# Other PSUM banks for the last rounds of a first attention, and its gate inputs normalised in two rounds

## The reference

```
x = x + xattn0(layernorm(x), ctx)    # 16 heads of 8, softmax over 128 keys, then wo and bo
x = x + ffn0(layernorm(x))           # 8 experts, top 2 of softmax(x @ gate_w)
x = x + xattn1(layernorm(x), ctx)    # 16 heads of 64, low-rank additions, 4 extra context tokens
x = x + ffn1(layernorm(x))           # 16 experts of 256, each takes its best 32 of 256 tokens
```

## Time and profile before

| | |
|---|---|
| time, median of 3 runs | 531.92 us (531.68 to 533.07) |
| profiled execution | 532.59 us, span 530.9 us |
| TensorE busy | 495.0 us, 93% of the span |
| VectorE busy | 397.5 us, 75% |
| ScalarE busy | 272.2 us, 51% |
| GpSimd busy | 235.7 us, 44% |
| first attention, rounds 12 to 17 | about 85 to 126 us of the span |

### The profile page before, as it was taken

One profiled execution on the slowest core, in us unless ns is written; L12 is line 12 of the kernel. 1 busy time (PEld: TensorE's weight loads), 2 busy tenths in 40 slices (PEclk: granted clock), 3 DMA queues, 4 the chain that ended last, 5 costly groups with the idle time before them and its releaser, 6 DMA issues.

```text
span 530.9 us, 13371 instructions
## 1 busy us (share of the span) xinstructions
PE 495.0 (93%) x5113; PEld 380.4 (72%) x5113; DVE 397.5 (75%) x1064; ACT 272.2 (51%) x728; POOL 235.7 (44%) x331
## 2 busy tenths in 40 slices
PE   5799998889999998999989999999999999999996
PEld 4467665546567776777768777778857897789895
DVE  6788998556687789777897897777986678536553
ACT  3366564445475564657545665555663544514332
POOL 5844553025365525556255454633312890081440
PEclk9699999899999999999999999999999999999999
DMA  8900000000001101111000000021110400001001
GB/s 227 220 4 4 2 2 2 2 1 7 4 0 32 32 2 33 32 32 32 2 2 1 3 1 3 3 62 45 39 41 1 120 1 2 0 4 41 2 2 41
DMA packets 21871, 14.47 MB, mean 27 GB/s; under 512 B 5928, under 2 KB 21136, under 8 KB 21808
## 3 DMA queue, kind: packets, MB, share of 16 engines
q1 hardware_dynamic: 20704, 13.31, 9.1%
q10 hardware_dynamic: 1104, 0.30, 0.3%
HBM read 12.30 MB, written 1.05 MB: 25 GB/s over the span
## 4 chain that ended last, share of the span: by engine, by line
PE 73%; DVE 20%; issue 3%; ACT 2%; DMA 1%; POOL 0%; SPq 0%; DVEq 0%
PE bank L1758 9%; PE bank L1767 5%; PE bank L1352 5%; PE bank L1521 5%; PE bank L1433 4%; PE bank L1528 4%; PE bank L1508 4%; PE bank L1690 4%; PE bank L1480 4%; PE bank L1500 4%; PE bank L1491 3%; PE bank L1774 3%; PE bank L1337 3%; PE bank L1579 3%; DVE negmax L756 2%
## 5 line engine op out<-in xcount | busy, mean ns | idle before, releaser
L496 POOL TENSOR_TENSOR work<-work,rsum 128x496 f32<-128x496 f32 x64 | 64.2, 1015 | 131.6 <-DVE rsum L774 131.6
L1128 ACT ACTIVATE work<-bank,negmax 128x124 f32<-128x124 f32 x256 | 72.7, 378 | 77.6 <-DVE ipa_s L758 77.6
L531 POOL TENSOR_SCALAR work<-work,slot 128x128 f32<-128x128 f32 x64 | 49.8, 804 | 48.1 <-DVE slot L849 29.3
L1758 PE MATMUL bank<-work 128*128 128x256 f32 x224 | 53.4, 381 | 0.0
L993 DVE SCALAR_TENSOR_TENSOR work<-work,bank 128x256 f32<-128x256 f32 x64 | 26.9, 420 | 32.9 <-ACT work L1280 32.7
L479 POOL TENSOR_TENSOR work<-work 128x512 f32<-128x512 f32 (+2 forms) x48 | 40.3, 839 | 14.1 <-DVE work L728 11.6
L1280 ACT ACTIVATE work<-bank 128x256 f32<-128x256 f32 x64 | 24.6, 384 | 40.5 <-PE bank L1758 29.0
L1758 PEld LDWEIGHTS bank<-work 128*128 128x128 f32 x224 | 40.3, 190 | 4.7 <-DVE work L996 0.2
L430 POOL TENSOR_TENSOR rstd<-veps,minus_half 128x1 f32<-128x1 f32 (+3 forms) x28 | 21.1, 754 | 49.3 <-DVE veps L573 49.2
L756 DVE TENSOR_REDUCE negmax<-bank 128x4 f32<-128x496 f32 x64 | 42.3, 662 | 0.0
L627 DVE TENSOR_REDUCE negmax<-bank 128x8 bf16<-128x1024 f32 x32 | 39.1, 1221 | 4.3 <-PE bank L1322 3.6
(11 more groups left out here) (197 smaller groups left out, 1086.3 us busy)
## 6 DMA issues: line engine op xcount, KB each, us to landing
work<-in_L_ffn_w_dram SPq DMA_DIRECT2D x42, 128.0 KB, 2.3
x_all<-in_x_dram SPq DMA_DIRECT2D x4, 256.0 KB, 5.5
out_dram<-x_all SPq DMA_DIRECT2D x4, 256.0 KB, 2.5
ctx_all<-in_ctx_dram SPq DMA_DIRECT2D x4, 192.0 KB, 5.7
ctx_all<-in_L_ffn_w_dram SPq DMA_DIRECT2D x6, 128.0 KB, 2.2
work<-in_L_xattn_Wq_dram SPq DMA_DIRECT2D x1, 512.0 KB, 6.4
work<-in_L_xattn_Wo_dram SPq DMA_DIRECT2D x1, 512.0 KB, 8.5
work<-in_L_ffn_We_dram SPq DMA_DIRECT2D x1, 512.0 KB, 6.0
```

The costliest lines, as they stand in the source:

```text
L496: pool.tensor_tensor(part, part, rsum1[:, b % 2, CH * n:CH * n + CH].unsqueeze(2).broadcast_to((128, CH, ORG)), ALU.mult).then_inc(Z.norm, 1)
L531: ins = pool.tensor_scalar(ohw_of(e)[:, k, :], count[:, :], slot[:, h, 0, k, e % E1:e % E1 + 1], slot[:, h, 1, k, e % E1:e % E1 + 1], ALU. ...
L1128: ins = act.activation(p1[:, b % 2, n, c, 0:ORG], blocks(bank[n])[:, c, 0:ORG], ACT.Exp, bias=negmax1[:, b % 2, CH * n + c:CH * n + c + 1])
L1758: mm = pe.matmul(halves(bank[4 + c])[:, n, :], up_weights(e, n, c), xgT[e // E1][:, :, e % E1, :], start=True, stop=True)
```

## The change

Spare rounds now go to 13 (SPARE 14). After them, round 14 uses bank 2 for both the turned maxima and the projection, round 15 bank 0, rounds 16 and 17 bank 7. values0 waits for VectorE's reads only in rounds 0 and 1. In exchange, TensorE waits ahead of project0 for the last user of each of these banks: in round 13 for ScalarE's copy of the turned gate inputs, in round 14 for the last maxima, in round 15 for the three copies by down_turned, in round 16 for the last exponentials. It also waits for VectorE's reads of the projections ahead of the next write into the same bank: head_logits(0) (bank 0), ffn(0, 0) (bank 2), fold(0) (bank 0), and inputs(0) (bank 7). head_input(0) is cut into two pairs: batches 0 and 1 are normalised in round 11, batches 2 and 3 in round 12, each pair behind the statistics and ahead of the reciprocal.

```diff
-        SPARE = 13
+        SPARE = 14
...
-            return TURN0[:, 128:256] if spare(b) else OUT0[:, 256:384]
+            return OUT0[:, 256:384] if b < FILL else TURN0[:, 128:256] if spare(b) else bank[2][:, 128:256]
...
-            return TURN0[:, 0:128] if spare(b) else OUT0[:, 384:512]
+            if b < FILL:
+                return OUT0[:, 384:512]
+            return (TURN0 if spare(b) else bank[{14: 2, 15: 0, 16: 7, 17: 7}[b]])[:, 0:128]
...
+                if b in (11, 12):
+                    head_input(0, 2 * (b - 11), 2 * (b - 10))
...
-            def head_input(j):
+            def head_input(j, first=0, end=4):
...
-                for k in range(4):
+                for k in range(first, end):
...
-                if b == 12:
-                    head_input(0)
...
-                if not spare(t + 1):
+                if t + 1 < FILL:
                     after(pe, A.negT_sb, min(t + 3, B))
                     after(pe, A.x_new, t)
...
+                    if b == 13:
+                        pe.wait_ge(F.xT, 1)
+                    if b == 14:
+                        pe.wait_ge(A.maxed, 2 * B)
+                    if b == 15:
+                        pe.wait_ge(W.downT, 3)
+                    if b == 16:
+                        pe.wait_ge(A.exp, 2 * B)
                     if there(y):
                         project0(y)
...
                 if b == 15:
-                    pe.wait_ge(A.maxed, 2 * B)
+                    pe.wait_ge(A.negT_sb, B)
+                    pe.wait_ge(A.x_new, 13)
                     pe.wait_ge(got.ffn0, 16)
...
                 if b == 13:
+                    spare_read(14)
                     head_logits(0, bank[0])
...
                 if b == 15:
-                    pe.wait_ge(W.downT, 3)
+                    pe.wait_ge(A.x_new, 14)
                     fold(0)
...
                     down_o_turn(1)
+                    pe.wait_ge(A.x_new, B)
                     inputs(0)
```

## The result

The changed kernel took 526.76 us (median of 6 runs, 525.35 to 528.84), the kernel before 532.5 us in the same rounds (6 runs, 531.68 to 533.6). The ratio is 0.9891, with a 95% interval from 0.9864 to 0.9918: 5.7 us less, between 4.4 and 7.2. Forecast were 6.15 us less and 525.8 us, in a range from 524.5 to 528.0.

A forecast was written before the change was run, and what follows sets the result against it. TensorE, busy 93% of the span, was taken as the bound, losing time to waits and half clock. Terms 2.15 + 1.5 + 0.45 + 0.85 + 0.95 + 0.45 - 0.2 = 6.15 us gave 525.8 us, range 524.5 to 528.0.

The forecast's parts named there:

- the clock's 1.5 us: Behind round 12's gate transposes: with the 2.52 us pause gone the clock stays full, 1.5 us saved.
- Inputs: Rounds 11 and 12: normalising in pairs ahead of the reciprocal starts the gate transposes 2.15 us earlier.
- Round 13's bank: Round 13, outputs in TURN0 (bank 0): values no longer wait for the turned maxima, 0.45 us saved.
- round 14's: Round 14, bank 2: values no longer need a copy by VectorE, 0.85 us saved.
- round 15's: Round 15, bank 0: TensorE waits for the residual only at fold(0), behind the values, 0.95 us saved.
- round 16's: Round 16, bank 7: the idle time ahead of the values goes, 0.45 us saved.
- new waits: Four new places of waiting for the banks: 0.2 us taken off the gain, between nothing and 0.5.
- The covers: Rounds 13 to 16: added waits or late work hide under other work; without round 13's cover up to 0.7 us lost.
- rival A: The clock falls once all the same, perhaps at second-attention pauses, costing 1.5 us: 527.3 us, chance 0.10.
- B (VectorE becomes the bound): Rounds 11 and 12: normalisations delay VectorE and the last rows' maxima, 1.5 us missing: 527.3 us, chance 0.07.
- C (swallowed later): A load with its own time holds the second attention or experts, so the end stays: 531.5 us, chance 0.03.
- D (falls in round after round): Second-attention pauses bring the clock down in six of sixteen rounds: slower, 534.8 us, chance 0.03.

The follow-up runs named there:

- all four in round 12: Changed kernel with all four gate inputs normalised in round 12 ahead of its reciprocal, none in round 11; ratio to before 0.9896.
- the banks alone: Changed kernel with its new banks, but the four gate inputs normalised behind round 12 as before; ratio to before 0.9929, profiled once more later.
- inputs alone: Kernel before with the gate inputs normalised in pairs in rounds 11 and 12 ahead of the reciprocal, banks as before; ratio 0.9941.
- the run with round 13 alone: Changed kernel with rounds 14 to 17 back in OUT0 with their waits, round 13 keeping TURN0; one profile, no time or ratio given.
- the filled pause: Kernel before with 16 identity transposes into bank 0 ahead of TensorE's wait for the four gate inputs; ratio to before 0.9991.
- the long one: Kernel with the new banks and inputs behind round 12, plus six VectorE scratch operations ahead of the inputs; ratio to before 1.0015.
- the faster version: Changed kernel with earlier second-attention input, 13 filling transposes in rounds 4 and 8, and o_up folds in banks 0 and 3; 524.94 us, ratio to before 0.9848.
- the later pauses filled: Changed kernel with 13 unread identity transposes ahead of the residual wait in rounds 4 and 8 of the second attention; ratio to before 0.9869.

## Why the prediction was right, and where it was not

The direction and the size were right. The waits in the sum were 0.8 us too small; the clock's 1.5 us came back in the first pair of profiles, but it is not a fixed term, and its share in the medians is not settled.

**The waits, by the changed kernel's table.** Inputs: 2.36 us where I had 2.15. Most of the difference is round 11, where I let 0.15 us through. The two normalisations start 0.2 us behind the statistics and the reciprocal 0.5 us behind them, so they take 0.5 and not 0.56 us; the reciprocal starts 5.10 us behind the anchor in both kernels. Round 12 even came 0.14 us earlier, since VectorE began its maxima 0.21 us behind the start of o0T (0.43 before). With all four in round 12, or with the banks alone, this is gone again; why two operations ahead of the reciprocal make the maxima behind it start sooner stays open. Round 13's bank 0.53 (I had 0.45), round 14's 0.97 (0.85), round 15's 1.02 (0.95), round 16's 0.54 (0.45). Round 13's is read between inputs alone and the run with round 13 alone (13.67 - 13.14), and the latter repeats the other three. The four are 3.06 instead of 2.70. I had taken each a little under the idle time of the earlier trace rows; it is the idle time and up to 0.1 us more. The 0.2 us that I took off for new waits were not there. Without the clock these terms are 5.4 us, where I had 4.65. The covers held: ScalarE's copy, down_turned's three copies and the late residual made nobody wait, and ScalarE's part of gate product 0 (105.68 to 106.82) ended in time for TensorE's next gate product at 106.88.

**The clock.** The step "Between the ends of nothing and 1.5 us I take 1.5" is borne out by the first pair of profiles (7.1 us to the end) and not with the changed kernel's second one (451.2 - 445.6 = 5.6 us). As the price of one fall 1.5 us is about right (1.5 in the filled pause, 1.6 in the long one, 1.5 in the changed kernel's second profile, 1.2 each in inputs alone). As a difference between medians it isn't a given, because the same pause was followed by a fall in one execution and not in the next, and other pauses were followed by one as well. I had argued that pauses of 0.95 and 2.0 us were not followed by any fall: that was one execution. In all thirteen profiled executions:

| pause of TensorE | executions with it | followed by a fall |
|---|---|---|
| 4.54 us, ahead of the gate transposes | 1 | 1 |
| 2.52 us, same place | 3 | 1 |
| 2.04 us, second attention, near 200 us | 11 | 2 |
| 2.04 us, same, near 270 us | 11 | 0 |
| 1.00 us, ahead of the first scores | 12 | 4 |
| 0.97 us, second attention, near 320 us | 13 | 0 |
| 0.95 us, ahead of the gate transposes at the stage's end (L1421 at 126.05 in the earlier trace rows) | 11 | 0 |

These are all eight falls. They began between 0.13 us before the end of the pause and 1.4 us behind it. Length alone doesn't sort them: 24 pauses of 0.95 and 0.97 us and 11 of 2.04 us had no fall, in the same executions in which those of 1.00 us had four.

With the clock taken out, the kernel before would need 449.7 us from the anchor, as its filled twin does, and the changed one needs 444.1. That is 5.6 us, of which the two measured groups of waits are 5.4. Whether the medians hold more than that, the record doesn't settle. The first comparison gave 5.7 us (4.4 to 7.2), the second, with the changed kernel's second profile, 6.7 us (5.1 to 8.6), and both intervals hold 5.6 as well as 7.1. By rival A, to which I gave 0.10, the clock goes on falling about once: one of the two profiles of the changed kernel has such a fall, the other none. By my own sign ("if the clock reads 0.50 anywhere past 30 us") the second would have spoken against me. The mean clocks point to fewer falls in the changed kernel. Values that a profile showed together with exactly one fall behind the start-up, 0.986, 0.995 and 0.996, stand in 31 of 54 executions of the kernel before and in 2 of 12 of the changed one. That is a hint and no count, since 0.990 was also seen with one fall, and with no fall at all the mean was 0.998 or 0.999 in four profiles, 0.992 in one and 0.989 in two, by what the record has of the start-up. So what the clock gave back on average stays open; these numbers name no value between the prediction's ends of nothing and 1.5 us.

**The rule of the Trainium skill.** Falls came in kernels with the old banks (the kernel before, and inputs alone at 141 and 206 us) as well as with the new ones. Five of the nine profiles with all the new banks have none (the changed kernel's first, both of banks alone, all four in round 12, the faster version), and the falls of the other four came at pauses that the old banks have too, or at one that was made longer. So nothing points to the rotation of banks. But small pauses, by which the Trainium skill's page "TensorE: Matmul & The Clock Gate" explains such falls in its section "A second HAM failure mode: psum-queue depth-cycling", can matter here: a pause of 1.00 us was followed by a fall in 4 of 12 executions, while those of 0.95 and 0.97 us were followed by none in 24. I had set the rule aside on the evidence of a single trace.

**The other rivals.** B (VectorE becomes the bound) is refuted by the 0.30 us at the transposes and by values without a bracket. C (swallowed later) by 451.2 - 444.1 = 7.1 us to the end, as much as at the first queries. D (falls in round after round) by the mean clocks, 0.989 to 0.999 in the changed kernel's twelve runs, where six falls at 0.003 each would leave 0.981 or less.

What stays open: what exactly makes the clock fall at a given pause in one execution and not in the next, how often it does, and so how much of the 1.5 us the median gets; thirteen profiles are few.

## What to carry to other kernels

Ahead of a wait of TensorE on VectorE, look at what VectorE does between the last input it had and the awaited result: four operations, moved in pairs ahead of one that itself waits for TensorE, made it start no later (5.10 us behind the anchor in both kernels) and gave 2.4 us. Where two small results share a PSUM bank with a large one, the idle time in front of the large one is what another bank gives back, round by round, if the bank's last reader is an instruction that ends earlier anyway. Don't take a stretch at half clock in one profile for a property of the kernel: compare behind an anchor, read the clock in several profiles, and put into the sum only the share of the price that they bear out. And read a gap between a pair of profiles and the medians against the interval first: 5.7 us became 6.7 when it was measured again.

## What the runs showed of the hardware

Behind the anchor the stage repeats to 0.02 us from execution to execution (39.85, 39.85 and, with the later pauses filled, 39.86 us to the first queries), and from the anchor to the end the two profiles of the banks alone, both without a fall, took 446.5 and 446.6 us, while the start-up differs by 4 us (78.20 to 82.20). So in these profiles the spread lies in the start-up and in the falls of the clock, which cost 1.2 us (two falls together 2.4, inputs alone) to 1.6 us each (the long pause), and two profiles with an anchor resolve about 0.1 us where ten runs resolve about 1.5.

The mean clock of a run leaves out the start-up where the record of the clock begins late. In the changed kernel's first profile it is 0.998, although its key matmuls took half again as long in the start-up as behind it (ns, shortest, median and longest; windows 18 to 27.5 and 28.5 to 40 us):

```profile
L1388 PE MATMUL bank<-cT_all,work x5: 421/421/439, 18.1 to 27.4; 96*128 96x128 f32 x5
...
L1388 PE MATMUL bank<-cT_all,work x4: 273/275/337, 32.9 to 38.2; 96*128 96x128 f32 x4
```

The profile of the banks alone, with a recorded stretch at half clock in its start-up, has the lower mean of 0.989.
